# A two-layer attention block on one core: the last third of the kernel in two halves of the tokens

## The reference

```
x1 = x  + attention(LN(x), ctx) @ w_out.T          32 heads in 8 key groups, masked
x2 = x1 + LN(x1) @ W_base.T + b + 0.5 * update     update: low-rank, masked, inverse Fourier
x3 = x2 + fake_quant(LN(x2)) @ fake_quant(ctx)     round and clip to 0..255
s  = LN(x3) in 4 streams of 256 features
logits = rms_norm(LN(x3)) @ [W_res; W_pre; W_post].T + base     16 + 4 + 4 a token
H    = g * sinkhorn(logits[0:16] as 4x4 / 0.1, 50 iterations) + (1 - g) * I
pre, post = softmax(logits[16:20]), softmax(logits[20:24])
y    = (sum_n pre[n] * s[n]) @ W_branch
out[i] = x3[i] + sum_j H[i,j] * s[j] + post[i] * y     i = 0..3
```

## Time and profile before

| what | value |
|---|---|
| median of three runs | 1085.72 us |
| the profiled execution | 1083.67 us |
| its span, first to last instruction | 1081.8 us |
| granted PE clock, mean | 0.984 |
| busy: PE, DVE, ACT, POOL | 96%, 81%, 61%, 9% of the span |
| feed-forward tiles 0 to 7 | 818 to 918 us |
| quantised product and logits | 918 to 964 us |
| stage_e | 964.4 to 1081.8 us |

### The profile page before, as it was taken

How to read it: one execution, slowest core, us unless ns; L and a number is a source line. 1 busy time by engine, 2 the same in 40 slices (tenths; PEclk the granted TensorE clock), 3 DMA queues, 4 the chain that set the end, 5 groups by cost and what they waited for, 6 DMA issues and landing times. The chain is left out here.

```text
span 1081.8 us, 20230 instructions
## 1 busy us (share of the span) xinstructions
PE 1036.7 (96%) x7188; PEld 783.9 (72%) x7192; DVE 874.7 (81%) x1880; ACT 663.5 (61%) x1126; POOL 92.7 (9%) x84
## 2 busy tenths in 40 slices
PE   8999999999999999999999999989999999956978
PEld 7878888777777777777777777765788887534647
DVE  5754444799999999999999999955774795879998
ACT  5322221498999889899989989942322114635837
POOL 0220011200000000000000000000003112400000
PEclk9999999999999999999999999999999999987989
DMA  8458879931123233212332321157415000000003
GB/s 335 171 195 281 264 254 259 324 106 42 39 74 73 73 68 73 51 36 63 73 73 68 73 60 34 36 209 251 130 59 170 0 0 1 1 1 1 1 1 155
DMA packets 55568, 112.95 MB, mean 104 GB/s; under 512 B 7724, under 2 KB 21164, under 8 KB 55388
## 3 DMA queue, kind: packets, MB, share of 16 engines
q1 hardware_dynamic: 55402, 112.10, 33.4%
q10 hardware_dynamic: 50, 0.16, 0.0%
q0 software_dynamic: 64, 0.00, 0.0%
HBM read 83.99 MB, written 27.26 MB: 103 GB/s over the span
## 5 line engine op out<-in xcount | busy, mean ns | idle before, releaser
L885 DVE CUSTOM_DVE_ANT_0 XS<-b_psS,b_mbias 128x1024 f32<-128x1024 f32 x256 | 311.0, 1215 | 0.6 <-PE b_psS L766 0.4
L840 ACT ACTIVATE XS<-XS,b_mins 128x1024 f32<-128x1024 f32 x256 | 295.8, 1155 | 10.8 <-DVE b_mins L885 10.2
L799 PEld LDWEIGHTS b_psT<-ident,XS 128*128 128x128 f32 x2048 | 230.0, 140 | 65.8 <-issue 47.6
L799 PE MATMUL b_psT<-ident,XS 128*128 128x128 f32 x2048 | 271.9, 276 | 1.6 <-ACT b_PT L848 1.6
L894 DVE COPY b_PT<-b_psT 128x512 f32<-128x512 f32 x256 | 176.9, 691 | 27.2 <-PE b_psT L799 25.6
L848 ACT COPY b_PT<-b_psT 128x512 f32<-128x512 f32 x256 | 149.5, 584 | 38.9 <-PE b_psT L799 30.9
L766 PE MATMUL b_psS<-XTh 128*128 128x512 f32 x512 | 156.1, 422 | 0.8 <-DVE b_mins L885 0.4
L780 PE MATMUL b_psO<-b_PT,XTh 128*32 128x256 f32 x1984 | 132.8, 385 | 0.0
L766 PEld LDWEIGHTS b_psS<-XTh 128*128 128x128 f32 x512 | 85.1, 189 | 18.8 <-DVE b_mins L885 8.2
L780 PEld LDWEIGHTS b_psO<-b_PT,XTh 128*32 128x32 f32 x1984 | 51.7, 109 | 42.1 <-issue 20.8
L416 ACT ACTIVATE a_oh<-a_psM 128x512 fp32r<-128x512 f32 x24 | 14.2, 595 | 81.7 <-PE a_psM L335 56.4
(11 more groups left out here) (267 smaller groups left out, 1619.2 us busy)
## 6 DMA issues: line engine op xcount, KB each, us to landing
XS<-in_ctx SPq DMA_DIRECT2D x16, 512.0 KB, 5.7
XTh<-QHd SPq DMA_DIRECT2D x32, 256.0 KB, 4.7
XTh<-QLd SPq DMA_DIRECT2D x32, 256.0 KB, 5.3
XS<-in_ctx_turned SPq DMA_DIRECT2D x8, 512.0 KB, 10.1
XS<-in_x SPq DMA_DIRECT2D x8, 512.0 KB, 11.5
a_wst<-in_L_xattn_w_q SPq DMA_DIRECT2D x8, 512.0 KB, 5.5
a_xn<-in_ctx_turned SPq DMA_DIRECT2D x8, 512.0 KB, 4.1
QHd<-a_oh SPq DMA_DIRECT2D x16, 256.0 KB, 5.2
```

The source lines that it names most:

```text
L799: last_t = pe.transpose(psT[:, kt, :], Pr[:, k % PR, kt * P:(kt + 1) * P], ident[:])
L840: act.activation(Pr[:, k % PR, :], Sc[:, k % 4, :], ACT.Exp, bias=mins[:, k % 4:k % 4 + 1], scale=-1.0, accum_out=sums[:, u, j:j + 1]).the ...
L885: dve.tensor_tensor_reduce(out=Sc[:, k % 4, :], in0=psS[:, k % 2, :], in1=mbias[:, qt, :], scale=1.0, scalar=3.4e38, op0=ALU.add, op1=ALU.min,
```

## The change

FFN tiles 0 to 3 run, then the quantised product and logits for these tiles, then the same for tiles 4 to 7. The first half's chain of Sinkhorn iterations (`one`) starts inside stage_cd: 29 half steps (`FIRST_ITERS = 14` iterations and the opening column step) are put between DVE's other work. In stage_e the two chains do 35 iterations together, chain one is finished (`sink` 2), and chain two does its last 14 alone. All four rows of tiles 0 to 3 are mixed by PE; tiles 4 to 7 are shared out as before. The rescaling is done once for each chain. In front of all this `keep_warm` goes from 14 to 5 matmuls, POOL takes half of the first mask tile, and PE weighs two of eight key tiles of the last unit at the end of stage_b, before the barrier. In the diff, the part from `turn_row` to the second half of `ffn(QT, 0)` is PE's, the part from `next_lo(1)` to `half_steps` DVE's.

```diff
+FIRST_ITERS = 14
-            keep_warm(pe, psM[:, 0, 0:P], ident, 14)
+            keep_warm(pe, psM[:, 0, 0:P], ident, 5)
...
+            end.weigh(pe, range(2))
-            end.weigh(pe)
+            end.weigh(pe, range(2, NK // 2))
+            end.weigh(pe, range(NK // 2, NK))
...
+            def turn_row(t):
+                pe.wait_ge(normed, t + 1)
+                pe.wait_ge(op_split, t + NT)
...
             def column_sums(b):
                 pe.wait_ge(q2_in[b], 16)
                 pe.wait_ge(sum_operands, 2 * (b + 1) + 1)
-                pe.wait_ge(op_split, 2 * NT)
+                pe.wait_ge(op_split, NT + QT + 1)
                 pe.wait_ge(col_ready, b)
...
+            for t in range(QT - 1):
+                turn_row(t + 1)
+                ffn(t, 0)
+                ffn(t, 1)
+            turn_row(QT)
+            ffn(QT - 1, 0)
+            column_sums(0)
+            turn_q(0)
+            ffn(QT - 1, 1)
+            turn_q(1)
+            column_sums(1)
+            product_q(0)
+            turn_q(2)
+            turn_weights()
+            product_q(1)
...
+            logits(0)
+            ffn(QT, 0, range(KT // 2))
+            turn_x(3)
+            turn_logits(0)
+            turn_row(QT + 1)
+            ffn(QT, 0, range(KT // 2, KT))
...
+            next_lo(1)
+            sum_parts(0, 0)
+            residual(0, 0, NT)
+            next_lo(2)
+            sum_parts(0, 1)
+            residual(1, 1, NT)
+            next_lo(3)
+            clip(0)
+            clip(1)
+            sum_parts(1, 0)
+            residual(2, 0, NT)
+            next_lo(4)
+            clip(2)
+            sum_parts(1, 1)
+            column_term(0)
+            residual(3, 1, NT)
+            column_term(1)
...
+            half_steps(0, 6)
+            residual(5, 1, NT, (6, 7))
...
         def pe_rows(t):
-            return 2 if t < NT - 1 else 1
+            return STREAMS if t < QT else 2 if t < NT - 1 else 1
...
             pe.wait_ge(post_added, NT)
-            pe.wait_ge(sink_near, LOOPS[2])
+            pe.wait_ge(sink, 1)
+            for t in range(QT):
+                lay_rows(t)
+            for t in range(QT):
+                done = mix_rows(t, done)
+                if t >= 1:
+                    lay_rows(t + QT - 1)
+            lay_rows(LAST)
+            for t in range(QT, NT):
+                done = mix_rows(t, done)
...
+            iterations(1, 4, [one, two])
+            recentre(4, one)
+            iterations(2, 9, [one, two])
+            recentre(9, two)
+            iterations(1, 14, [one, two], near=True)
+            finish(14, one, 0)
+            iterations(2, 16, [two])
+            finish(16, two, 1)
```

More of the change, by code:

```diff
@@ L1431, in _ @@
[L1431 to L1440, removed]
-            turn_weights()
-            for t in range(NT):
-                if 1 < t + 1 < NT:
+                pe.wait_ge(q_kept, QT if g < 2 else NT)
@@ new lines, in _ @@
+            ffn(QT, 0, range(KT // 2, KT))
+            logits(1)
+            ffn(QT, 1, range(KT // 2))
+            turn_logits(1)
+            ffn(QT, 1, range(KT // 2, KT))
+            for t in range(QT + 1, LAST):
+                turn_row(t + 1)
+                ffn(t, 0)
+                ffn(t, 1)
+            ffn(LAST, 0)
+            turn_q(QT)
+            ffn(LAST, 1)
+            turn_q(QT + 1)
+            product_q(QT)
+            for t in range(QT + 1, NT):
+                if t + 1 < NT:
@@ L1460, in _ @@
+            turn_logits(3)
         @block.scalar
@@ L1522, in _, with next_hi, next_norm, ffn_std @@
             std(LAST * 3 + 2)
[L1524 to L1531, removed]
+            def next_hi(t):
+                norm_hi(t % 2, t + 1, t + (NT + 1))
+            def next_norm(t):
+                norm(t, t % 2, t - 1)
+            def ffn_std(t):
+                std(t * 3 + (3 * NT + 2))
             def scale_y(t):
@@ L1713, in _, with next_lo @@
             quant_parameters()
-            def ffn_body(j, last):
-                for u in range(2):
-                    t = j * 2 + u
-                    if not (last and u == 1):
-                        norm_lo(1 - u, t + (NT + 2))
-                    if j > 0:
-                        sum_parts(j - 1, u)
-                    residual(t, u, NT)
+            def next_lo(t):
+                norm_lo(t % 2, t + (NT + 1))
             def sum_parts(b, n):
@@ L1808, in _ @@
+            next_lo(7)
+            clip(4)
+            clip(5)
+            half_steps(8, 12)
+            residual(6, 0, NT, (12, 13))
+            clip(6)
+            half_steps(14, 20)
+            residual(7, 1, NT, (20, 21))
+            clip(7)
+            combine(4)
+            half_step(22)
+            combine(5)
+            half_step(23)
+            combine(6)
+            half_step(24)
+            combine(7)
+            half_step(25)
             dve.wait_ge(x_turned, NT)
             dve.tensor_copy(xT[:, KT // 2:KT, slot(NT - 1)], psX(NT - 1)[:, KT // 2:KT, :]).then_inc(x_kept_low, 1)
-            sum_logits(0)
@@ L2101, in _ @@
             dve.wait_ge(exps, 3)
-            cuts = [NT * c // CHAINS for c in range(CHAINS + 1)]
-            groups = [(c, slice(cuts[c], cuts[c + 1])) for c in range(CHAINS)]
-            def times(n, axis, factor, out, src):
-                for c, g in groups:
-                    f = factor[:, g, :].unsqueeze(axis).to_broadcast([P, g.stop - g.start, STREAMS, STREAMS])
-                    dve.wait_ge(chain, n + c)
-                    dve.tensor_tensor(out[:, g], src[:, g], f, ALU.mult).then_inc(chain, 1)
@@ L2134, in iterations @@
+            def iterations(loops, done, chains, near=False):
+                size = 3 * len(chains)
+                n = done - len(chains) + 1
+                dve.wait_ge(chain, done)
                 with dve.Fori(0, loops):
                     for i in range(PER_LOOP):
-                        if near is not None and i == 2:
-                            dve.sem_inc(near, 1)
-                        row_step(n + i * 2 * STEP)
-                        col_step(n + i * 2 * STEP + STEP)
-                    dve.sem_inc(chain, -2 * STEP * PER_LOOP)
@@ L2144, in _ @@
+            dve.sem_inc(chain, 1)
+            step(1, [two], False)
+            iterations(1, 4, [one, two])
             dve.wait_ge(soft_step, 3)
```

605 lines of the change are left out of this document (361 added, 244 removed).

## The result

The changed kernel takes 1111.23 us (median of 4 runs, 1108.71 to 1113.13) beside 1084.69 for the kernel before (1082.1 to 1085.82, 4 runs): a ratio of 1.0245, 95% interval 1.0227 to 1.0263. It is slower by 26.5 us, and the forecast was 1110.

The account below looks back on a forecast made before the run. PE was taken to bound feed-forward to logits, and DVE's iterations, then PE's mixing, stage_e. Early edits -3.5, stage_cd +18.7 and stage_e +10.5 on 1083.7 gave 1109.4, taken as 1110 us, range 1095 to 1119.

Parts of the forecast that it names:

- The bound, and where it would pass to: PE bounds feed-forward to logits, DVE's iterations stage_e; after the change PE's mixing ends last, over 20 us behind DVE's.
- Waits of the first half, 15.1: Stage_cd, feed-forward of tiles 0 to 3: PE waits for DVE's lengthened list, 15.1 us together, the largest wait 9.3.
- The end of the stage, 3.6: Stage_cd's end: four products instead of eight pipelined, filling and emptying alone, last half steps: 3.6 us later.
- The half steps under tiles 4 to 7 at nothing, and 2.3 for the last three: Stage_cd: early half steps cost nothing under PE's work on tiles 4 to 7; three before the last logits cost 2.3 us.
- Stage_e, 10.5: Stage_e gets 10.5 us longer, bounds 8 and 13: PE has 92 mixing matmuls behind the branch instead of 60.
- Early edits, -3.5: Before the feed-forward: less warming, half mask on POOL, key tiles weighed before the barrier save 3.5 us, bounds 0 and 4.
- The three parts (1.6, 0.6, 1.3): Savings in us: fewer warming matmuls 1.6, half mask on POOL 0.6, two key tiles weighed before the barrier 1.3.
- The sum: Whole kernel: 1083.7 - 3.5 + 18.7 + 10.5 = 1109.4 us for an execution like the profiled one, taken as 1110.
- A: Rival: orders fit, stage_e's end stays on DVE with PE mixing by 52 us into the stage: 1072 us, 5%.
- B: Rival: stage_cd takes no waits, only stage_e counts: 1095 us, 12%.
- C: Rival: stage_e's cost is hidden, stage_cd's is not: 1086.5 us, no difference that can be told, 3%.
- D: Rival: waits compound, leaving PE's clock at 1.2 GHz through tile 3 and before the branch: 1119 us, 15%.

Follow-up runs that it names:

- e1_rows2: Changed kernel, but DVE mixes two rows of every full tile again and PE the other two: 1101.41 us, ratio 1.0150.
- e2_colsum_pe: Changed kernel, but PE instead of DVE makes the row sums of the quantised context, with bf16 ones: 1099.3 us, ratio 1.0130.
- e4_first7: Changed kernel, but 7 instead of 14 iterations of the first half run early, the other 7 in stage_e: 1110.31 us, ratio 1.0233.
- e3_colsum_late: Changed kernel, but column_sums(0) stands later on PE's list, behind the second half of ffn(3) and turn_q(1): 1114.04 us, ratio 1.0267.
- e8_no_early: Changed kernel with its three early edits (warming products, half mask, split weighting) undone: 1114.9 us, ratio 1.0270.
- e5_early: Kernel before with only the three early edits (fewer warming products, half mask on POOL, split weighting): 1080.45 us, ratio 0.9962.

## Why the prediction was right, step by step

- **The bound, and where it would pass to**: right. PE's first mixing record stands 78.9 us into the stage (81 forecast), DVE's last mixing instruction ends 20.9 us before PE's (over 20 forecast), the gap in front of the first column sums is 9.51 (9.3) and is ended by DVE's low part with a reduction in front, and stage_e opens at 985.6 (near 980, 983.2 worked out). e1_rows2 and e2_colsum_pe show each by removing it.
- **Waits of the first half, 15.1**: PE's rows have 9.5 + 0.8 + 1.7 = 12.0 for what was forecast as 9.3 + 2.6 + 3.2. The last wait is smaller because the products behind the gap ran at the lower clock and used its time up: they started at 873.19 and PE was back at the column sums at 884.50, which is where the working put it (883.8, plus the 1.0 by which this execution was late). The loss of 2 to 3 us was so in fact covered, but it was some 2 and lay in the column sums and the turn behind them; the half layer, which was to run slower too, ran at full clock (granted 1.00 from 877.4 to 883.1).
- **The end of the stage, 3.6**: 1.5 too small. The wait for `keep_q(5)` is there (1.4, 1.1 forecast), but not in the working are the waits on ACT's `d_xT` 1.1 and `d_lt` 0.5 and on DVE's `XR` 0.6 and `colterm` 0.5. They lie behind the second column sums, up to which the working is right to 0.3 us, and with 2.7 us they are more than the 1.5 needs; which of them the opening of stage_e feels was not isolated. e2_colsum_pe keeps all but `colterm` unchanged: they belong to the halved product and not to the row sums.
- **The half steps under tiles 4 to 7 at nothing, and 2.3 for the last three**: right in the experiment that takes away 14 of them, the last three among these (e4_first7): feed-forward to logits gets shorter by 2.3, the price of the three alone.
- **Stage_e, 10.5**: 8.3 in the trace. The branch ended 1.8 us earlier than the shifted time of before (71.8 against 73.6), and PE's mixing took 43.4 us where 44.4 were reckoned. Of the 1.8, 1.4 are the branch's second product: it ran at the lower clock in the trace that gave the 73.6 (3.30 us to the next product) and at full clock here (1.89). Where it ran slow in the changed order too, stage_e took 127.3 and 127.1 us (e3_colsum_late, e4_first7), which is 9.9 and 9.7 more than before. Before, the branch was not on the chain that ended last, so the stage did not feel this; now it does. The mechanism holds; the low bound was 8.
- **Early edits, -3.5**: the profiled execution shows +1.0, and its late stage_a accounts for 2.4 of the difference, not for all of it; by the timed runs the edits give 3.8 to 4.1 us in the kernel before (medians; ratio 0.9962) and 2.7 to 3.7 in the changed one. The size is right, and the single trace would have denied it. The three parts (1.6, 0.6, 1.3) were not measured one by one.
- **The sum**: 1083.7 - 3.5 + 18.7 + 10.5 came to 1109.4. By measured terms, -4 + 20.2 + 8.3 = 24.5, against 26.5 between the medians; the profiled executions differ by 29.5. The two terms that were off, +1.5 and -2.2, nearly cancelled. That the total lies within 1.2 us of the median is so in part luck; stages of the same code differ by as much between executions.
- **Rivals**: A would have needed PE at the mixing by 52 us; it came at 78.9. B fell with the 9.5 us wait, and its price was good: with the reductions gone the time is 1099 (1095 forecast, of which 3.5 us are the sums that PE then makes). C fell: stage_e took 8.3 us more, not 12.4 less. D fell: from 820 to 982 us of the changed kernel only the long gap costs the clock, and only until 877.4; behind the waits of 1.12 and 0.56 us the granted clock stayed at 1.00.

## What to carry to other kernels

Before work is moved to an engine earlier in its list, write out that engine's list with durations and look up each result behind the moved piece that another engine needs: the 30 us of reductions had all their time hidden in the old order, and cost 12 us in the new one though none of them grew. A wait removed on the waiting engine's side (e3_colsum_late) comes back under another name; moving the long instruction on the list that delivers helps a little, taking it off that list helps wholly. And where two engines share a pool of work at the end, set the share by when each of them can start, not by which half of the data is ready: PE mixing 3, 3, 3 and 2 rows of the first four tiles instead of all four was worth 11 us of the stage. And time work that was moved into a gap against less of it: half of the early iterations brought nothing.

## What was not expected of the hardware

- DVE's clip of a tile took 0.64 to 0.69 us in nine places of the traces of before and changed kernel and 1.8 to 2.9 in the other seven. Each of the seven began while an instruction of GpSimd ran and ended 0.5 to 0.6 us behind that one's end; each of the nine began with GpSimd idle. One pair of the changed kernel:

```profile
872.88 2.35 POOL L2029 TENSOR_TENSOR XR<-XR,c_wst 128x1024 f32<-128x1024 f32 x1 [13.67 <-ACT c_src L1566]
```
```profile
873.97 1.81 DVE L1873 TENSOR_SCALAR d_y<-d_y 128x1024 f32<-128x1024 f32 x1 [1.04 <-ACT d_y L1629]
```

So the clip looks as if it waited for GpSimd's instruction, but no run takes that instruction away.

- A stage that no version touches ended anywhere from 199.4 to 203.1 us in eleven profiled executions. With differences below 1% a stage has to be timed from its own opening; two executions' spans can't be subtracted. Even so timed, shared code differed: by up to 3.5 us from stage_a's end to tile 7 of the projections over the nine kernels with the early edits, and by 1.6 us in stage_e (the changed kernel and e3_colsum_late).
- The same wait may or may not cost the clock. The weighting product follows 2.51 us of idling both in the kernel before and in e8_no_early, where it is the same; its 64 records took 5.35 us and 3.66. The stretch from 709 to 712.5 us (columns as in the earlier trace rows) shows the granted clock at 0.56 in the first, near the 1.2 GHz level, and at 1.00 in the second:

```profile
709.00:712.50 3.50, 3.26 (x34) 2.15 (x37) 2.13 (x2) 3.22 (x4) 0.00 (x0) 0.56 0.02 5
```
```profile
709.00:712.50 3.50, 3.32 (x64) 2.39 (x64) 2.17 (x2) 3.27 (x4) 0.00 (x0) 1.00 0.02 5
```

With the product split, all nine profiled executions show 1.07 and 2.80 us for the two parts. That the split keeps the clock up, beside taking work from behind the barrier, would explain why the edits gave more than the 1 to 2 us expected of e5_early; two executions without it are too few to call it shown. The branch's second product is another such place: 2.05 us or 3.63 behind the same wait of 1.17 (e4_first7).
